# Routing of half the tokens moved from the expert loop into the attention before it, in a two-layer transformer kernel

## The reference, cut to what matters

```python
z = layernorm(x); z0 = z
for _ in range(2):                                   # LOOPS
    z_norm = rmsnorm(z, norm_w)
    scores = softmax(z_norm @ router_w)              # 8 experts
    topk_vals, topk_idx = top_k(scores, 2)           # then normed to sum 1
    z = z + sum over e of cw[:, e] * (silu(z_norm @ w1[e]) * (z_norm @ w3[e])) @ w2[e]
x = x + z
```

## Time and profile before

| | |
|---|---|
| device time, median of 3 | 2308.4 us |
| profiled execution: span, no other time of it is given | 2763.4 us |
| TensorE, busy | 2109.4 us (76%) |
| VectorE, busy | 1847.5 us (67%) |
| ScalarE, busy | 1458.9 us (53%) |
| GpSimd, busy | 1221.4 us (44%) |
| granted TensorE clock, mean | 0.886 of full |
| DMA packets | 224611, 226.95 MB |

### The profile page before, as it was taken

How to read it: one execution, slowest core, us unless ns; L and a number is a source line. 1 busy time by engine, 2 the same in 40 slices (tenths; PEclk the granted TensorE clock), 3 DMA queues, 4 the chain that set the end, 5 groups by cost and what they waited for, 6 DMA issues and landing times. The chain is left out here.

```text
span 2763.4 us, 47500 instructions
## 1 busy us (share of the span) xinstructions
PE 2109.4 (76%) x14679; PEld 1039.5 (38%) x14679; DVE 1847.5 (67%) x5421; ACT 1458.9 (53%) x3354; POOL 1221.4 (44%) x1710
## 2 busy tenths in 40 slices
PE   5999999999899899999999464665747585556662
PEld 1222222222256444444444243443535353344441
DVE  8999999999767788888888453544434344344324
ACT  1888888888833477777777222332314232233231
POOL 5433434332102577777775344244443524443434
PEclk9999999999999899999999677887859677777876
DMA  6535444354101133333332122221212222222322
GB/s 161 138 99 142 116 124 131 101 147 116 40 1 46 48 94 94 89 76 72 94 94 49 57 61 65 60 69 59 76 56 74 67 66 64 65 68 62 88 75 82
DMA packets 224611, 226.95 MB, mean 82 GB/s; under 512 B 34032, under 2 KB 187504, under 8 KB 224368
## 3 DMA queue, kind: packets, MB, share of 16 engines
q1 hardware_dynamic: 152432, 164.62, 22.4%
q0 software_dynamic: 16384, 33.59, 4.1%
q10 hardware_dynamic: 55552, 25.71, 3.2%
HBM read 96.48 MB, written 125.76 MB: 80 GB/s over the span
## 5 line engine op out<-in xcount | busy, mean ns | idle before, releaser
L702 ACT ACTIVATE mid_PT<-mid_ps 128x512 f32<-128x512 f32 (+2 forms) x1792 | 913.6, 568 | 257.7 <-PE mid_ps L583 249.8
L785 DVE TENSOR_REDUCE mid_nmax<-mid_ps 128x1 f32<-128x512 f32 (+2 forms) x1280 | 776.2, 657 | 61.8 <-PE mid_ps L562 36.7
L562 PE MATMUL mid_ps<-KT,QT 48*128 48x512 bf16 (+3 forms) x2048 | 604.6, 351 | 68.3 <-DVE mid_nmax L785 49.7
L1395 PE MATMUL moe_ps<-moe_w,moe_xinT 128*128 x638 | 393.0, 702 | 315.6 <-issue 171.2
L583 PE MATMUL mid_ps<-QT,KT 64*128 64x512 bf16 (+3 forms) x2048 | 562.0, 346 | 2.6 <-ACT mid_PT L702 2.2
L1547 DVE TENSOR_TENSOR moe_h<-moe_ps,moe_sg 128x256 f32<-128x256 f32 x319 | 134.7, 422 | 518.4 <-ACT moe_sg L1459 279.9
L599 PE MATMUL mid_ps<-mid_PT,vv 128*32 128x512 f32 (+3 forms) x4096 | 464.5, 526 | 15.8 <-POOL mid_PT L914 12.0
L1450 ACT ACTIVATE moe_xinT<-moe_ps,norm_w 128x128 f32<-128x128 f32 x319 | 116.8, 366 | 677.4 <-remote 318.3
L1506 POOL DMA_INDIRECT rows_in<-moe_xn,moe_scat_idx x256 | 246.7, 964 | 462.0 <-DVE moe_scat_idx L1695 388.0
L562 PEld LDWEIGHTS mid_ps<-KT,QT 48*128 48x128 bf16 x2048 | 158.9, 94 | 585.5 <-DVE mid_nmax L785 397.6
L1519 POOL DMA_INDIRECT moe_yg<-rows_out,moe_gat_idx x256 | 245.1, 957 | 249.1 <-issue 122.1
(11 more groups left out here) (265 smaller groups left out, 3025.7 us busy)
## 6 DMA issues: line engine op xcount, KB each, us to landing
l_spread<-mid_slots SPq DMA_DIRECT2D x128, 384.0 KB, 5.5
rows_in<-mid_blank SPq DMA_DIRECT2D x64, 512.0 KB, 4.3
QT<-l_spread SPq DMA_DIRECT2D x128, 192.0 KB, 4.3
KT<-l_spread SPq DMA_DIRECT2D x128, 192.0 KB, 5.2
moe_xin<-rows_in SPq DMA_DIRECT2D x319, 64.0 KB
rows_out<-moe_y ACTq DMA_DIRECT2D x319, 64.0 KB
x<-in_L_attn_x_dram SPq DMA_DIRECT2D x8, 512.0 KB, 6.6
QT<-mid_mrows SPq DMA_DIRECT2D x256, 6.0 KB
```

The lines of the kernel that those rows point to most:

```text
L562: mm = pe.matmul(ps[:, bank, n_keys * a:n_keys * (a + 1)], QT[rows, par, pair, i * P:(i + 1) * P], KT[rows, par, pair, 0:n_keys], start=Tr ...
L702: act.activation(weights_of(r, i, heads), ps[:, ring(S2, n - 2, k), 0:widths[i] * len(heads)], ACT.Exp, scale=scale).then_inc(exp_done, 1)
L785: dve.tensor_reduce(to, of, X_AXIS, ALU.max, negate=True).then_inc(s1_used, 1)
L1395: mm = pe.matmul(ps[:, GU[v % BANKS], :], xinT[:, v % 2, :], w13[:, bass.ds(expert(v), 1), :].rearrange("p a f -> p (a f)"), start=True, s ...
```

## The change

Passes 0 to 3 (k < `EARLY` = 4) leave the expert block and are done by a new class `Early` inside the steps of the second attention. A pass k takes 16 steps, from 4 steps before step 21 + 12k to 11 after it; each engine's step function calls `Early` at fixed slots (`off` is the step counted from 21 + 12k, so off = 0 has n % 4 = 1). VectorE does the statistics and the choices as before; the layernormed z and the scaled xn are made by ScalarE instead, one tile at a time. z of each pass is saved to DRAM by SP and loaded again in the expert block. GpSimd issues the 64 scatters of the passes, 4 at a time: in the steps 34, 38, ..., 62 and in all of 66 to 71, 56 in all; 8 are left for the start of the expert block. Its new waits are z_ready, t_made, r_made and so on, between the engines' parts of a pass. The work tensors of the passes lie in free places of the attention's buffers. The buffer `PT` outlives the attention, and the expert weights are loaded into it by SP as soon as the last weighted sum is done. Tables of units 0 and 1 are made at the start of the expert block, then the tile loop starts at once; SP waits for the new semaphore `rows_made`, raised before the gather indices are done. `begin` and `transfers` are written anew.

```diff
+EARLY, SPAN, OPEN = 4, 12, 21
+class Early:
+    def at_step(self, n):
+        for k in range(EARLY):
+            if -4 <= n - (OPEN + SPAN * k) < 12:
+                yield k, n - (OPEN + SPAN * k)
+    def sync(self, sp, n):
+        for k, off in self.at_step(n):
+            if off == 4:
+                sp.wait_ge(self.z_ready, 2 * k + 2)
+                sp.dma_start(self.saved[k], self.z.rearrange("p t d -> p (t d)")).then_inc(self.z_saved, 16)
+    def tensor(self, pe, n, use, bank, free):
+            if (off, use) in ((1, 3), (2, 2)):
...
+                for t in range(IT // 2):
+                    mm = pe.transpose(bank[:, t * P:(t + 1) * P], self.z[:, IT // 2 * (off - 1) + t, :], self.w["ident"][:, :])
+            if (off, use) == (5, 3):
...
+                for t in range(IT):
+                    mm = pe.matmul(bank[:, t * EXPERTS:(t + 1) * EXPERTS], self.zT[t // 4][:, (t % 4) * P:(t % 4 + 1) * P],
+                                   self.w["router"][:, :], start=True, stop=True)
+            if (off, use) == (9, 3):
...
+    def scalar(self, act, n, u, bank):
+            z_at = {(1, 4): 0, (1, 5): 1, (1, 7): 2, (1, 9): 3, (1, 11): 4, (1, 13): 5, (2, 4): 6, (2, 6): 7}
+            xn_at = {(8, 8): 0, (8, 14): 1, (9, 4): 2, (9, 5): 3, (9, 7): 4, (9, 9): 5, (9, 11): 6, (9, 13): 7}
...
+    def vector(self, dve, n, u, bank, x_added):
+            if (off, u) in ((-4, 3), (-3, 6)):
...
+            if (off, u) == (-1, 2):
+                c.link(dve.tensor_scalar(m2, var, 1e-5, None, ALU.add))
+                rsqrt_seed(c, rstd, m2)
+            if (off, u) == (-1, 5):
+                cubic_root(c, rstd, m2, tmp)
+            if (off, u) == (-1, 8):
+                cubic_step(c, rstd, tmp)
+            if (off, u) == (-1, 11):
+                c.link(newton(c, rstd, m2, tmp))
+            if (off, u) == (-1, 14):
+                c.link(dve.tensor_tensor(var, var, rstd, ALU.mult))
+                dve.scalar_tensor_tensor(nmean, mean, -1.0, rstd, ALU.mult, ALU.mult).then_inc(self.scaled, 1)
...
+            if (off, u) == (5, 14):
+                dve.wait_ge(self.r_made, k + 1)
...
+            if (off, u) == (7, 2):
+                choose(c, sel[:, 0, :, :], lg, m["mx"], m["key"], m["best"], self.falling[:, :])
...
+            if (off, u) == (7, 10):
+                dve.wait_ge(self.second_ready, k + 1)
+                choose(c, sel[:, 1, :, :], sh2, m["second"], m["key"], m["best"], self.falling[:, :])
...
+            if (off, u) == (9, 14):
+                dve.wait_ge(self.k_made, k + 1)
...
+    def scatters(self, n):
+        if n < OPEN + 12 or n >= STEPS + 8:
+            return range(0)
+        shares = [4 if m % 4 == 2 or m >= STEPS + 2 else 0 for m in range(OPEN + 12, n + 1)]
+        done = sum(shares[:-1])
+        return range(done, min(done + shares[-1], 2 * IT * EARLY))
@@ attention, gpsimd: behind the additions to x, ahead of the masks
+                if early:
+                    for i in early.scatters(n):
+                        early.scatter(pool, i)
@@ middle, sync
             sp.wait_ge(zeroed, 16 * STEPS)
+            sp.wait_ge(second.signals["av_done"], STEPS)
+            w13_in(sp)
@@ experts
-    EARLY = 2
-    begin = {2: 0, 3: 14, 4: 29, 5: 47, ...}
+    begin = {4: 0, 5: 14, 6: 28, 7: 42, 8: 60, 9: 84, 10: 104, 11: 125, 12: 145, 13: 165, 14: 185, 15: 206,
+             16: 228, 17: 244, 18: 256, 19: 278, 20: 292}
+    transfers = ("s4 s5 g8 s6 s7 g9 s8 g10 s9 g11 s10 g12 s11 g13 s12 g14 s13 g15 g16 s14 s15 g17 g18 "
                  "g19 g20 g21 g22 g23").split()
@@ experts, sync
-            sp.dma_start(w13[:, :, 0:FF], ins["L1_ffn_w1"].rearrange("e d f -> d e f")).then_inc(w_in, 16)
...
+            for k in range(EARLY):
+                sp.wait_ge(early.z_saved, 16 * EARLY)
+                sp.dma_start(z[:, tiles_of(k):tiles_of(k) + IT, :].rearrange("p t d -> p (t d)"), early.saved[k]).then_inc(z_in, 16)
...
-                    sp.wait_ge(tables, u + 1)
+                    sp.wait_ge(rows_made, u + 1)
@@ experts, gpsimd
+            left = sum(len(early.scatters(n)) for n in range(STEPS + 8))
+            for i in range(left, 2 * IT * EARLY):
+                early.scatter(pool, i)
@@ experts, vector
+            for u in range(UNITS):
+                if first_of[u] + sizes[u] <= EARLY:
+                    make_tables(u)
             run(tile, side, 0)
```

More of the change, by code:

```diff
@@ L383, in fills, with choose @@
             dve.tensor_tensor(each, each, self.wsum[:, k, :, :].unsqueeze(3).to_broadcast([P, 2, 8, HD]), ALU.add)
+IT = 8
+GROUPS = BATCHES * TILES // IT
+SIZES = [1] + [2] * (GROUPS - 1) + [1]
+FIRST_OF = [sum(SIZES[:u]) for u in range(len(SIZES))]
+UNIT_OF = [max(u for u in range(len(SIZES)) if FIRST_OF[u] <= k) for k in range(LOOPS * GROUPS)]
+CAP = IT * max(SIZES) * P
+EARLY, SPAN, OPEN = 4, 12, 21
+def choose(c, dst, scores, top, key, best, falling):
+    dve = c.eng
+    c.link(dve.tensor_tensor(key, scores, top.unsqueeze(2).to_broadcast([P, IT, EXPERTS]), ALU.is_equal))
+    c.link(dve.tensor_tensor(key, key, falling.unsqueeze(1).to_broadcast([P, IT, EXPERTS]), ALU.mult))
+    c.link(dve.tensor_reduce(best, key, X_AXIS, ALU.max))
+    c.link(dve.tensor_tensor(dst, key, best.unsqueeze(2).to_broadcast([P, IT, EXPERTS]), ALU.is_equal))
@@ L392, in __init__, with attention @@
         self.signals = signals
-def attention(nc, ctx, tag, ps, shared, x, w, kept, center, causal, after=None, opening=None):
+def attention(nc, ctx, tag, ps, shared, x, w, kept, center, causal, after=None, opening=None, early=None):
     scale = 1.0 if causal else float(DIM) ** -0.5
@@ L1038, in swiglu_int, with middle @@
                  center_groups=CENTER_GROUPS)
-def middle(nc, x, w, sides0, sides1, kept, center, rows_in, opening):
+def middle(nc, x, w, sides0, sides1, kept, center, rows_in, big, early, w13_in, opening):
     with ExitStack() as ctx:
@@ L1057, in middle @@
             "nrest": ([P, 2, 2 * TILES], F32), "mrows": ([P, 2, P], BF16), "rec": ([P, TILES * 4, 2], F32),
-            "ao": ([P, 2, TILES, DIM], F32), "PT": ([P, 2 * 4 * TILES * SEQ], F32)}.items()}
+            "ao": ([P, 2, TILES, DIM], F32), "ffn_xn": ([P, TILES, DIM], F32)}.items()}
+        shared["PT"] = big
+        shared["ffn_xnT"], shared["ffn_sg"] = (early.xn[:, a, :, :].rearrange("p (a t) d -> p a (t d)", a=2) for a in range(2))
+        early.place(big, [shared["ffn_xn"][:, :, :].rearrange("p t d -> p (t d)"), blank[:, :]], zeroed)
         spare, at = shared["PT"], 2 * 4 * P * TILES * (TILES + 1) // 2
@@ L1073, in middle @@
         after = After(one, ffn.signals)
-        second = attention(nc, ctx, "l1_", ps, shared, x, sides1, kept, center, causal=True, after=after)
+        second = attention(nc, ctx, "l1_", ps, shared, x, sides1, kept, center, causal=True, after=after, early=early)
         late = one["late"]
@@ L1160, in _ @@
             second.vector(dve, (0,), range(4, 16))
+            early.fills(dve)
             second.vector(dve, range(1, STEPS + 8))
@@ L1181, in experts @@
     STAGES = 20
-    sizes = [1] + [2] * (GROUPS - 1) + [1]
+    sizes, first_of, unit_of = SIZES, FIRST_OF, UNIT_OF
     UNITS = len(sizes)
-    first_of = [sum(sizes[:u]) for u in range(UNITS)]
     tiles_in = [2 * IT * n + EXPERTS - 1 for n in sizes]
@@ L1649, in side @@
                 if s in (16, 17):
-                    if s == 16 and k >= 3:
+                    if s == 16 and k >= EARLY + 3:
                         dve.wait_ge(scattered[k % 3], 16 * 2 * IT * (k // 3))
@@ L1808, in two_layers @@
                           wo=square["L1_attn_Wo"])
-            middle(nc, x, w, layer0, layer1, kept, center, rows_in,
+            middle(nc, x, w, layer0, layer1, kept, center, rows_in, big, early, load_experts,
                    lambda sb, sem: Opening(sb, sem, x, x_dram, x_in, w["small"], small_in, kept, center, deep))
-        z = sb("z", [P, BATCHES * TILES, DIM], F32)
-        experts(nc, x, z, w, tri, ins, out.rearrange(rows, p=P), rows_in)
+        experts(nc, x, z, w13, w2, w_in, out_done, early, w, tri, ins, out.rearrange(rows, p=P), rows_in)
 _INS = ['L0_attn_x', 'L0_attn_Wq', 'L0_attn_Wk', 'L0_attn_Wv', 'L0_ffn_w_gate', 'L0_ffn_w_up', 'L0_ffn_w_down',
```

355 lines of the change are left out of this document (273 added, 82 removed).

## The result

The change makes the kernel slower: 2380.8 us (median of 4 runs, 2376.7 to 2383.1) against 2308.3 us (4 runs, 2307.6 to 2309.2), ratio 1.0312, 95% interval [1.030, 1.0325]. I had forecast 2324, a loss of 16 us; it is 72. The profiled execution after took 2376.7 us, its span 2374.9, so its sums are made against 2308.3 + 68.4.

What follows compares the result with a forecast made beforehand. Prediction: VectorE and TensorE nearly full in the attentions, tiles and GpSimd together bounding the 708 us expert loop. Terms -41 + 22 + 70 - 35 = +16 us gave 2324 us; range 2264 to 2385, the forecast's own 2305 to 2345.

Steps and rivals of the forecast that it cites:

- Part 1: Start of the last stage: the first expert tile comes after 10 us instead of 51.3, a gain of 41 us.
- Part 2: Attention's lead-out: 24 scatters on GpSimd in steps 66 to 71 delay the next stage, a cost of 22 us.
- Part 3: Second attention: four passes, each 25 us of VectorE with blocked small operations, lengthen it by 70 us.
- Part 4: Expert loop: two passes and 48 scatters leave it, a gain of 35 us, middle of 10 and 60.
- 0.73: Second attention: us by which a batch gets longer per us of VectorE work, other engines' share included.
- the upper bound: Second attention: 116 us for four passes, if all 29 operations each wait for a whole big GpSimd operation.
- its lower end: Expert loop: about 10 us gained if tiles bound it, from TensorE work and a wait at unit 1's start.
- The 455 us between profile and runs: Profiled execution 2763.4 against 2308.4 us: the difference lies in the expert loop's stalls, leaving 708 us of loop for the runs.
- Rival 1: Second attention has room, so the passes cost 25 us there: 2279 us in total, faster; chance 0.31.
- Rival 2: Second attention: every two-input VectorE operation is blocked, costing 116 instead of 70 us: 2370 us; chance 0.13.
- Rival 3: Expert loop: GpSimd alone bounds it, so the gain is 60 instead of 35 us: 2299 us; chance 0.13.

Runs made afterwards that it cites:

- two_late: Changed kernel with two early passes instead of four, opened at step 49, router matmuls 64 columns wide, loop order of the kernel before: 2299.7 us, 0.9968 of the kernel before.
- long-loop sets: Sets of runs in which the unchanged kernel before takes 2763 to 2773 us, where other sets have 2308 to 2311 us.
- two_middle: The kernel of two_late with its two early passes opened at step 45 instead of 49: ratio 1.0012 to the kernel before.

## Why the prediction was wrong

- **Part 1, the start (-41): right.** 10.05 us from the stage's start to the first tile, as summed.
- **Part 2, the lead-out (+22): right, with one term missing.** GpSimd's last scatter ended 1663.5 - 1614.7 = 48.8 us behind the mark, as summed (1570.3 - 1521.6), and taking the 24 scatters away gave 21.8 us back. The other 4.6 of the 26.6 us are GpSimd's queue ahead of the next stage, 4.9 us, where the prediction had 0.3. (By reported spans this part would be 14.8 us, not 14.)
- **Part 3, the attention (+70): the mechanism named was right, a term was left out.** 93.2 us, of which 22.7 in the router's steps and 70.5 in the others. That the others come to the forecast 70 is luck, two errors that cancel: VectorE's added busy time was 454.1 - 384.5 = 69.6 us from step 17 to 64, 18.3 a pass, where the prediction put 25 into its product (21.3 of them busy, the rest gaps and waits), but it lengthened the attention by 1.0 us per us, not 0.73, which holds for operations that aren't blocked. The failed step is the one on TensorE: 1.5 us of VectorE's time "for its waits on the router and count matmuls, which TensorE issues only one slot earlier", which put TensorE's time at nothing, with 2 us for it in the upper bound alone. The router's 16 instructions stand in the steps in which TensorE was busy 8.93 of 9.40 us; they cost 2.7 to 2.9 us by their length and about as much again with the fallen clock, 5.7 a pass. (ScalarE's idle time in the earlier trace rows is 2.0 to 3.2 us a step, not the 1.5 to 2.7 of the text; nothing hangs on it.)
- **Part 4, the loop (-35): wrong, its lower end was the answer.** "Since both bound it about equally, 35 us, middle": the gain was 10 (9 against *two_late*). That both bound it was borne out (half of added GpSimd work shows), but from this one can't take the middle: the 60 us taken off GpSimd's order became 51 us of waiting for the tiles' outputs. This step, 25 us, has the largest share in the miss.
- The 455 us between profile and runs weren't a matter of profiling: long-loop sets have them in every run. That they lay in the loop was right, and so was its length (708; 705.4 and 706.1 in the profiles of *two_late* and *two_middle*). In the profile of the kernel before, TensorE, VectorE and ScalarE stand still together for over 4 us 28 times in the loop, 269 us in all; in *two_late* twice, 19 us.
- Rival 1 (25 us in the attention) failed by 68. Rival 2 (116 us there) came nearest in the total, 2370 for 2381, but not by its mechanism: the blocked operations made the steps longer by 70 us, the router's matmuls on TensorE did the rest. Rival 3 (GpSimd alone) would have had -60 in the loop, for -10.

Of the 52 us that the forecast missed in the profiled run, 28 lie in attention and lead-out and 25 in the loop.

## What to carry to other kernels

Moving small work into a stage that is "only" 84% busy costs about its full length if it comes as linked small operations beside another engine's big ones; count them, and look for the form that isn't blocked or the stretch where the other engine rests. Count every engine's share of the moved work against that engine's busiest step, not against the stage's mean. Where two engines bound a loop together, taking work off one of them is worth its lower bound until the trace shows that nothing it then waits for is late.
